# A tile's probabilities turned by two DMA transposes, one for the high and one for the low halves

## The chip, the core and the metric

The kernel runs on one core of a Trainium2 chip. The core has a matmul engine (TensorE, PE in the profile, its weight loads PEld), VectorE (DVE), ScalarE (ACT), GpSimd (POOL) and SyncE (SP), which issues the DMAs; 16 DMA engines move the data. The metric is the device time of one execution in microseconds (us).

## What is computed

Eight batches of 56 query rows of 256 numbers pass two cross-attention layers (16 heads of 128, 1500 context rows and one bias row each), a two-layer MLP, and a gated third cross-attention, the audio attention (16 heads of 16, the context normalised first, with a mask). The core of the reference, with its setup left out:

```python
def _cross_attention(q_in, kv_in, wq, bq, wk, bk, wv, bv, wo, bo, bias_k, bias_v):
    ...
    logits = jnp.einsum('bqhk,bthk->bhqt', qh, kh) / scale
    weights = jax.nn.softmax(logits, axis=-1)
    ctx = jnp.einsum('bhqt,bthk->bqhk', weights, vh).reshape(b, q_len, H * K)
    return ctx @ wo + bo
...
res = x
h = _layer_norm(x, ln1_scale, ln1_offset)
x = res + _cross_attention(h, xf_1, wq1, bq1, wk1, bk1, wv1, bv1, wo1, bo1, bias_k1, bias_v1)
res = x
h = _layer_norm(x, ln2_scale, ln2_offset)
x = res + _cross_attention(h, xf_2, wq2, bq2, wk2, bk2, wv2, bv2, wo2, bo2, bias_k2, bias_v2)
h = _layer_norm(x, ln_mlp_scale, ln_mlp_offset)
h = jax.nn.gelu(h @ w_fc1 + b_fc1, approximate=False) @ w_fc2 + b_fc2
...
a = _layer_norm(audio_kv, ln_gamma, ln_beta)
...
scores = jnp.einsum('bhtd,bhsd->bhts', Q, K) * scale
scores = jnp.where(mask, scores, jnp.float32(-jnp.inf))
attn = jax.nn.softmax(scores, axis=-1)
out = jnp.einsum('bhts,bhsd->bhtd', attn, V)
...
return hidden_states + jnp.tanh(gate) * out
```

## The kernel before

Numbers that enter a matmul are split in a high and a low half of 16 bits, and a product is made of three matmuls (high by high, high by low, low by high). In the first two attentions the queries are first taken through the keys' weights, so that scores and averages are made with the context itself. The 16 x 56 = 896 rows of heads and queries of a batch are 7 tiles (RT) of 128 rows; 8 batches make 56 tiles a layer (TILES). The 1500 context rows are 12 blocks (NT) of 128, the last of 92.

A tile t goes through these steps, each engine with its own order written out by hand:

1. TensorE makes the scores (`scores`), 3 parts of 6 matmuls and a one-column one, in three PSUM banks; odd and even tiles have their own.
2. VectorE takes the maxima (`maximum`, `row_maximum`, L1347, L1378), ScalarE the exponentials (`exponentiate`, L1071), into `prob`.
3. ScalarE writes the high half of the probabilities into `ph[:, i, 0:TC]` (`probs_high`, L1080), VectorE the low half into `ph[:, i, TC:2*TC]` (`probs_low`, L1403); i is t % 2.
4. SyncE turns both halves, 24 blocks of 128 x 128, by one DMA transpose into `pT` (`turn_probs`, L468).
5. TensorE makes the average (`weigh`): 12 blocks with three matmuls each, 36 in all.
6. ScalarE and VectorE write the average's halves (`average_high` L1089, `average_low` L1297), and SyncE turns them by a transpose of 4 blocks into the queries' place (`turn_average`, L476).

TensorE's loop over x runs scores of tile x and then the average of tile x - 2 (LAG). VectorE's slot x makes the maxima of tile x, with the low half of tile x - 1 between its first and its second part. SyncE's slot x turns tile x - 1, then the average of tile x - 3, and then issues loads of the context: DMAs of one queue, issued in this order, each behind the waits of those ahead. After tile 55 ScalarE waits for both last transposes before it splits four weight slices (L1039, L1263 on VectorE), since their place holds `ph` and `pT`. Then the column of the bias row goes round through memory (`tokT`, `scratch`, `ptok`), and the output projection begins.

The audio attention has 7 tiles for each of 8 batches as well. There `audio_maximum` (L1354) adds the mask and takes the maximum, `audio_exponentiate` is L1124, `audio_high` (L1133) writes `aph[:, i, 0:TC]`, `audio_low` (L1372) the low half, `turn_audio` (L508) turns both into `probT`, and `audio_average` makes 24 matmuls for a window of four heads (224 columns), four windows a batch. Between them run the units (keys and values of the next batch: TensorE, then L1117 and L1411), whose keys are turned by `turn_keys` (L499), 12 blocks at a time. SyncE's slot y holds the keys, the probabilities of tile y - 1, a piece of context (L445) and, in the slot of tile 4, the next batch's mask (`mask_load`, L460), right behind the transpose of tile 3. ScalarE turns the mask into a row (`mask_row`, L1138, and `mask_addend`, L1144) in the slot of tile 5, with small steps of VectorE between (L1436 to L1445), and VectorE's maximum of tile 6 comes after them.

## Time and profile before

| what | us |
|---|---|
| median of 3 runs | 1602.12 (1599.8 to 1603.47) |
| the profiled execution | 1609.13 |
| its span, from the first to the last instruction | 1607.4 |
| TensorE busy | 1470.9 (92%) |
| VectorE busy | 1020.2 (63%) |
| ScalarE busy | 833.2 (52%) |
| GpSimd busy | 480.5 (30%) |
| DMA engines, mean share | 74% in the queue of the kernel's DMAs |

The first attention runs from about 72 to 519 us, the second from 644 to 1093, the audio attention from 1208 to the end; projections, norms and the MLP lie between. A busy TensorE is at work for its whole span, and only what shortens its waits there can shorten the run; where it is idle, the row tells who released it. Times of a timeline count from the span's start.

### The profile page before, as it was taken

How to read it: one execution, taken by the hardware profiler on the slowest of the kernel's cores; microseconds unless marked ns; L12 is line 12 of the kernel's file. 1: busy time of each engine (PE TensorE's matmuls, PEld its weight loads, DVE VectorE, ACT ScalarE, POOL GpSimd, SP SyncE). 2: the span in 40 equal slices, each digit the busy share in tenths (PEclk: the TensorE clock that was granted, in tenths of full speed). 3: DMA queues.
4: the chain of work that ended last, by engine and by line, in shares of the span. 5: the costliest groups of instructions: out<-in, count | busy, mean ns of one | idle time of the engine just before them, and what ended most of it. 6: DMA issues, size and time to landing. Idle time of an engine off the chain costs nothing.

```text
span 1607.4 us, 24281 instructions
## 1 busy us (share of the span) xinstructions
PE 1470.9 (92%) x9170; PEld 889.3 (55%) x9170; DVE 1020.2 (63%) x2150; ACT 833.2 (52%) x1437; POOL 480.5 (30%) x456
## 2 busy tenths in 40 slices
PE   7989999999998989899999999998988887898875
PEld 3356666666665333566666666663443444444443
DVE  6755555556555347656666666653467787898885
ACT  4644455544454336455445554443345666666663
POOL 4424233423331200333342334200014444434300
PEclk9999999999999889999999999997999999999998
DMA  5198988988897210798889889884115989999886
GB/s 197 51 197 183 174 172 181 188 156 183 178 187 143 81 65 14 173 183 168 178 179 180 171 176 189 155 166 117 53 30 116 185 174 183 196 192 180 168 146 126
DMA packets 664704, 246.50 MB, mean 153 GB/s; under 512 B 637452, under 2 KB 638972, under 8 KB 664588
## 3 DMA queue, kind: packets, MB, share of 16 engines
q1 hardware_dynamic: 664588, 244.95, 74.2%
q8 instruction: 73, 1.20, 0.3%
q14 instruction: 43, 0.35, 0.1%
HBM read 84.94 MB, written 0.52 MB: 53 GB/s over the span
## 4 chain that ended last, share of the span: by engine, by line
PE 78%; DVE 10%; DMA 5%; ACT 3%; SPq 2%; issue 1%; ACTq 0%; DVEq 0%
PE SC L684 44%; PE PV L684 34%; DVE prob L1354 2%; DVE qc L1372 2%; SPq L508 2%; DVE core L1411 2%; DMA core<-qc 2%; DMA mask<-in_mask_dram 2%; DMA core<-core 1%; ACT rowbuf L1138 1%; DVE core L1403 1%; DVE core L1263 0%; ACT qc L1133 0%; DMA qc<-core 0%; ACT prob L1071 0%
## 5 line engine op out<-in xcount | busy, mean ns | idle before, releaser
L684 PE MATMUL PV<-core 128*128 128x256 f16 (+1 forms) x4800 | 546.6, 273 | 40.1 <-DMA core<-qc 16.4
L684 PEld LDWEIGHTS PV<-core 128*128 128x128 f16 x4800 | 463.7, 99 | 111.9 <-issue 19.3
L1071 ACT ACTIVATE prob<-SC,nmax 128x500 f32<-128x500 f32 x336 | 223.9, 675 | 430.7 <-DVE nmax L1378 430.7
L684 PE MATMUL SC<-ctxT,qc 128*128 128x500 f16 x2016 | 443.1, 374 | 2.6 <-DVE qc L1282 2.6
L1347 DVE TENSOR_REDUCE mx<-SC 128x1 f32<-128x500 f32 x336 | 225.0, 670 | 328.2 <-PE SC L684 328.2
L684 PEld LDWEIGHTS SC<-ctxT,qc 128*128 128x128 f16 x2016 | 195.5, 97 | 210.1 <-DVE qc L1282 3.5
L1403 DVE SCALAR_TENSOR_TENSOR core<-prob,core 128x1500 f16<-128x1500 f32 x112 | 200.0, 1786 | 8.2 <-ACT core L1080 8.2
L616 POOL CAST ctxT<-stage 128x750 f16<-128x750 f32 x64 | 53.1, 830 | 465.2 <-DMA stage<-in_ctx_t_dram 240.7
L1080 ACT ACTIVATE core<-prob 128x1500 f16<-128x1500 f32 x112 | 162.9, 1454 | 3.5
L684 PE MATMUL SC<-ctxT 128*128 128x512 f16 x576 | 143.0, 395 | 14.5 <-DVE core L1411 14.4
L684 PE MATMUL SC<-qc 128*128 128x512 f16 x480 | 118.8, 394 | 40.1 <-DVE mx L1354 40.1
L1124 ACT ACTIVATE prob<-prob,nmax 128x1500 f32<-128x1500 f32 x56 | 86.4, 1543 | 46.4 <-DVE nmax L1358 46.4
L1133 ACT ACTIVATE qc<-prob,rsc 128x1500 f16<-128x1500 f32 x56 | 86.4, 1544 | 42.6 <-DVE rsc L1365 29.1
L636 POOL CAST ctxT<-stage 128x768 f16<-128x768 f32 x32 | 27.6, 861 | 270.7 <-DMA stage<-in_ctx_p_dram 145.0
L1354 DVE CUSTOM_DVE_ANT_0 prob<-SC,rowbuf 128x1500 f32<-128x1500 f32 x56 | 95.9, 1712 | 18.7 <-PE SC L684 18.7
L1372 DVE SCALAR_TENSOR_TENSOR qc<-prob,rsc,qc 128x1500 f16<-128x1500 f32 x56 | 100.8, 1799 | 10.9 <-ACT qc L1133 10.9
L616 POOL CAST core<-stage 128x768 f16<-128x768 f32 x64 | 56.2, 878 | 169.2 <-DMA stage<-in_ctx_nat_dram 169.2
L684 PEld LDWEIGHTS SC<-ctxT 128*128 128x128 f16 x576 | 57.4, 101 | 89.2 <-issue 29.8
L618 POOL TENSOR_TENSOR core<-stage,core 128x768 f16<-128x768 f32 x64 | 105.1, 1643 | 5.1
L618 POOL TENSOR_TENSOR ctxT<-stage,ctxT 128x750 f16<-128x750 f32 x64 | 101.8, 1590 | 5.1
L684 PEld LDWEIGHTS SC<-qc 128*128 128x128 f16 x480 | 46.2, 99 | 101.4 <-issue 53.8
L1411 DVE SCALAR_TENSOR_TENSOR core<-SC,rstd,core 128x256 f16<-128x256 f32 x192 | 83.3, 476 | 18.2 <-ACT core L1117 18.2
(138 smaller groups left out, 1364.5 us busy)
## 6 DMA issues: line engine op xcount, KB each, us to landing
stage<-in_ctx_nat_dram SPq DMA_DIRECT2D x64, 384.0 KB, 3.9
stage<-in_ctx_t_dram SPq DMA_DIRECT2D x64, 375.0 KB, 3.5
stage<-in_ctx_p_dram SPq DMA_DIRECT2D x32, 384.0 KB, 3.8
core<-in_wq_dram SPq DMA_DIRECT2D x8, 512.0 KB, 3.6
core<-in_wk_dram SPq DMA_DIRECT2D x8, 512.0 KB, 3.7
core<-in_wv_dram SPq DMA_DIRECT2D x8, 512.0 KB, 4.2
core<-in_wo_dram SPq DMA_DIRECT2D x8, 512.0 KB, 4.4
qc<-core SPq DMA_TRANSPOSE x144, 2.5
```

Source lines behind the costliest of these rows:

```text
L616: nc.gpsimd.tensor_copy(hi, src).then_inc(split_hi, 1)
L618: nc.gpsimd.tensor_tensor(lo, src, hi, ALU.subtract).then_inc(stage_free, 1)
L684: return nc.tensor.matmul(o, a, c, start=start, stop=stop, skip_group_check=skip)
L1071: nc.scalar.activation(prob[:, i, c * CW:c * CW + w], SETS[i][c][:, 0:w], ACT.Exp, bias=nmax[:, i, :], accum_out=sum3[:, i, c:c + 1]).then ...
L1080: nc.scalar.activation(ph[:, i, 0:T], prob[:, i, 0:T], ACT.Copy, scale=UP).then_inc(ph_hi, 1)
L1124: nc.scalar.activation(prob[:, i, 0:T], prob[:, i, 0:T], ACT.Exp, bias=nmax[:, i, :], accum_out=sum3[:, i, 0:1]).then_inc(as_exp, 1)
L1133: nc.scalar.activation(aph[:, i, 0:T], prob[:, i, 0:T], ACT.Copy, scale=rsc[:, y % 4, 1:2]).then_inc(aph_hi, 1)
L1347: nc.vector.tensor_reduce(mx3[:, t % 2, c:c + 1], SETS[t % 2][c][:, 0:w], AX_X, ALU.max)\
L1354: nc.vector.tensor_tensor_reduce(out=prob[:, i, 0:T], in0=scores_of(y), in1=maskb[:, b % 2, :], scale=1.0, scalar=-3.0e38, op0=ALU.add, op ...
L1372: nc.vector.scalar_tensor_tensor(aph[:, i, TC:TC + T], prob[:, i, 0:T], rsc[:, y % 4, 1:2], aph[:, i, 0:T], ALU.mult, ALU.subtract).then_i ...
L1403: nc.vector.scalar_tensor_tensor(ph[:, i, TC:TC + T], prob[:, i, 0:T], UP, ph[:, i, 0:T], ALU.mult, ALU.subtract).then_inc(ph_lo, 1)
L1411: ins = nc.vector.scalar_tensor_tensor(lo[:, i, :, :], src[:, i, :, :], rstd[:, n:n + 1], hi[:, i, :, :], ALU.mult, ALU.subtract)
```

## The change

`ph` and `aph` are turned by two transposes of 12 blocks instead of one of 24. SyncE issues the one of the high halves as soon as ScalarE has written them (`ph_hi`, `aph_hi`), then waits for the low halves and issues the other. Each has its own semaphores (`pth_full`, `ptl_full`, `apth_full`, `aptl_full`). TensorE's average waits for the high ones, runs all matmuls with them (24 of 36, in the audio stage 12 of 24), then waits for the low ones and runs the rest. ScalarE's wait before it overwrites a high half is for the high transpose alone, and VectorE gets the wait for the low one.

```diff
@@ def turn_probs(t): @@
-                sp.wait_ge(ph_lo, t + 1)
+                sp.wait_ge(ph_hi, t + 1)
                 if t >= 2:
                     sp.wait_ge(pv_done, t - 1)
-                sp.dma_start_transpose(pT[:, i, :, :], ph[:, i, :]).then_inc(pt_full[i], 16)
+                sp.dma_start_transpose(pT[:, i, 0:NT, :], ph[:, i, 0:TC]).then_inc(pth_full[i], 16)
+                sp.wait_ge(ph_lo, t + 1)
+                sp.dma_start_transpose(pT[:, i, NT:2 * NT, :], ph[:, i, TC:2 * TC]).then_inc(ptl_full[i], 16)
@@ def turn_audio(y): @@
-                sp.wait_ge(aph_lo, y + 1)
+                sp.wait_ge(aph_hi, y + 1)
                 if b > 0:
                     sp.wait_ge(apv_done, NW * (b - 1) + LAST_WINDOW[s] + 1)
-                sp.dma_start_transpose(probT[:, :, s * P:(s + 1) * P], aph[:, i, :]).then_inc(apt_full[i], 16)
+                sp.dma_start_transpose(probT[:, 0:NT, s * P:(s + 1) * P], aph[:, i, 0:TC]).then_inc(apth_full[i], 16)
+                sp.wait_ge(aph_lo, y + 1)
+                sp.dma_start_transpose(probT[:, NT:2 * NT, s * P:(s + 1) * P], aph[:, i, TC:2 * TC])\
+                    .then_inc(aptl_full[i], 16)
@@ def weigh(l, x): @@
-                pe.wait_ge(pt_full[i], 16 * (t // 2 + 1))
+                pe.wait_ge(pth_full[i], 16 * (t // 2 + 1))
                 if t >= 2:
                     pe.wait_ge(av_lo, t - 1)
                 for j in range(NT):
                     w = width(j)
-                    for n, (pi, ci) in enumerate(((0, 0), (1, 0), (0, 1))):
-                        ins = mm(PV[i][:, 0:D], pT[0:w, i, pi * NT + j, :], nat[0:w, par, ci, j, :],
-                                 j == 0 and n == 0, j == NT - 1 and n == 2)
+                    for ci in range(2):
+                        mm(PV[i][:, 0:D], pT[0:w, i, j, :], nat[0:w, par, ci, j, :], j == 0 and ci == 0, False)
+                pe.wait_ge(ptl_full[i], 16 * (t // 2 + 1))
+                for j in range(NT):
+                    w = width(j)
+                    ins = mm(PV[i][:, 0:D], pT[0:w, i, NT + j, :], nat[0:w, par, 0, j, :], False, j == NT - 1)
                 ins.then_inc(pv_done, 1)
@@ def audio_average(b, w): @@
-                for i in range(2):
-                    pe.wait_ge(apt_full[i], 16 * ((y + 2 - i) // 2))
...
-                for j in range(NT):
-                    r = width(j)
-                    for i in range(2):
+                for i in range(2):
+                    for k in range(2):
+                        pe.wait_ge((apth_full, aptl_full)[i][k], 16 * ((y + 2 - k) // 2))
+                    for j in range(NT):
+                        r = width(j)
                         ins = mm(PV[w % 2][:, 0:WR], values(NT * b + j, w)[0:r, :],
                                  probT[0:r, i * NT + j, w * WR:(w + 1) * WR], j == 0 and i == 0, j == NT - 1 and i == 1)
@@ ScalarE, probs_high(t); audio_high(y) likewise with apth_full @@
                 if t >= 2:
-                    act.wait_ge(pt_full[i], 16 * (t // 2))
+                    act.wait_ge(pth_full[i], 16 * (t // 2))
@@ ScalarE, attention(l), x == TILES @@
-                            act.wait_ge(pt_full[i], 16 * (TILES // 2) * (l + 1))
+                            act.wait_ge(pth_full[i], 16 * (TILES // 2) * (l + 1))
+                            act.wait_ge(ptl_full[i], 16 * (TILES // 2) * (l + 1))
@@ VectorE, probs_low(t); audio_low(y) likewise with aptl_full @@
                 dve.wait_ge(ph_hi, t + 1)
+                if t >= 2:
+                    dve.wait_ge(ptl_full[i], 16 * (t // 2))
```

On SyncE's queue, the start of the first layer's attention, before: the transposes of tiles 0 to 3 (`core<-core`), with context and weights between, and the first turned averages (`qc<-core`).

```order
L421 DMA core<-in_wv_dram 128x1024 [waits w_lo]
L468 DMA_TRANSPOSE core<-core 128x24x128 [waits ph_lo]
L445 DMA stage<-in_ctx_nat_dram 128x768 [waits stage_free] x2
L421 DMA core<-in_wo_dram 128x1024 [waits w_lo]
L468 DMA_TRANSPOSE core<-core 128x24x128 [waits ph_lo]
```

The same place now:

```order
L423 DMA core<-in_wv_dram 128x1024 [waits w_lo]
L470 DMA_TRANSPOSE core<-core 128x12x128 [waits ph_hi]
L472 DMA_TRANSPOSE core<-core 128x12x128 [waits ph_lo]
L447 DMA stage<-in_ctx_nat_dram 128x768 [waits stage_free] x2
L423 DMA core<-in_wo_dram 128x1024 [waits w_lo]
L470 DMA_TRANSPOSE core<-core 128x12x128 [waits ph_hi]
L472 DMA_TRANSPOSE core<-core 128x12x128 [waits ph_lo]
```

Two transposes stand where one stood; nothing has changed its place.

On TensorE, tile 0's average in the first layer (`PV<-core`), behind the scores of tile 2, before:

```order
L684 MATMUL SC<-ctxT,qc 128x500 [waits exp_done]
L684 MATMUL SC<-ctxT,qc 128x500 x5
L684 MATMUL SC<-one,rowbuf 128x1
L684 MATMUL PV<-core 128x256 [waits pt_full0,stage_free]
L684 MATMUL PV<-core 128x256 x35
```

And now:

```order
L691 MATMUL SC<-ctxT,qc 128x500 x5
L691 MATMUL SC<-one,rowbuf 128x1
L691 MATMUL PV<-core 128x256 [waits pth_full0,stage_free]
L691 MATMUL PV<-core 128x256 x23
L691 MATMUL PV<-core 128x256 [waits ptl_full0]
L691 MATMUL PV<-core 128x256 x11
```

The 36 matmuls have been parted into 24 behind the high transpose and 12 behind the low one.

On SyncE's queue in the audio stage, the slots of tiles 3 and 4 of a batch (`qc<-core` are the keys, `core<-qc` the probabilities, `stage` a piece of context), before:

```order
L499 DMA_TRANSPOSE qc<-core 128x12x128 [waits as_score,m_lo]
L508 DMA_TRANSPOSE core<-qc 128x24x128 [waits apv_done,aph_lo]
L445 DMA stage<-in_ctx_p_dram 128x768 [waits stage_free]
L499 DMA_TRANSPOSE qc<-core 128x12x128 [waits as_score,m_lo]
L508 DMA_TRANSPOSE core<-qc 128x24x128 [waits apv_done,aph_lo]
L460 DMA mask<-in_mask_dram 128x1500 [waits mask_ready]
L499 DMA_TRANSPOSE qc<-core 128x12x128 [waits as_score,m_lo]
```

And now:

```order
L503 DMA_TRANSPOSE qc<-core 128x12x128 [waits as_score,m_lo]
L512 DMA_TRANSPOSE core<-qc 128x12x128 [waits apv_done,aph_hi]
L514 DMA_TRANSPOSE core<-qc 128x12x128 [waits aph_lo]
L447 DMA stage<-in_ctx_p_dram 128x768 [waits stage_free]
L503 DMA_TRANSPOSE qc<-core 128x12x128 [waits as_score,m_lo]
L512 DMA_TRANSPOSE core<-qc 128x12x128 [waits apv_done,aph_hi]
L514 DMA_TRANSPOSE core<-qc 128x12x128 [waits aph_lo]
L462 DMA mask<-in_mask_dram 128x1500 [waits mask_ready]
L503 DMA_TRANSPOSE qc<-core 128x12x128 [waits as_score,m_lo]
```

The mask still stands behind tile 3's low half, now with 12 blocks instead of 24 directly ahead of it.

## Rows read from the trace of the kernel before

**Rows 1.** The page, its first line.

```profile
span 1607.4 us, 24281 instructions
```

**Rows 2.** Windows: stretch, length, busy us (instructions) by engine, clock, DMA share, GB/s.

```profile
200.00:300.00 100.00, 100.00 (x710) 68.19 (x709) 55.99 (x129) 50.76 (x104) 36.04 (x30) 1.00 0.88 177
1400.00:1500.00 100.00, 83.55 (x483) 46.60 (x482) 81.88 (x163) 68.79 (x77) 46.25 (x58) 0.97 0.96 188
```

**Rows 3.** Line L499, the keys' transposes: issue ns min/median/max, then landing.

```profile
L499 SPq DMA_TRANSPOSE qc<-core x32: 1391/1432/2553, 1172.0 to 1539.9; - x32
...
DMA to landing us min/median/max: 3.6/4.5/6.2
```

**Rows 4.** Windows amid a lone 24-block and a lone 12-block transpose.

```profile
84.30:85.30 1.00, 0.00 (x0) 0.00 (x0) 0.15 (x1) 1.00 (x5) 0.00 (x0) 1.00 1.15 212
...
1174.00:1174.50 0.50, 0.34 (x2) 0.22 (x3) 0.50 (x2) 0.50 (x1) 0.00 (x0) 1.00 1.17 216
```

**Rows 5.** Timeline, both layers' first tiles: start, length, engine, line, what [idle before <-releaser].

```profile
80.59 1.72 DVE L1403 SCALAR_TENSOR_TENSOR core<-prob,core 128x1500 f16<-128x1500 f32 x1 [1.33 <-ACT core L1080]
...
88.09 6.94 PE L684 MATMUL PV<-core 128*128 128x256 f16 x36 [4.41 <-DMA core<-core]
...
652.89 2.93 DVE L1403 SCALAR_TENSOR_TENSOR core<-prob,core 128x1500 f16<-128x1500 f32 x1 [1.33 <-ACT core L1080]
...
657.22 0.16 DVE L1378 TENSOR_REDUCE nmax<-mx 128x1 f32<-128x3 f32 x1
...
661.51 6.95 PE L684 MATMUL PV<-core 128*128 128x256 f16 x36 [5.53 <-issue]
...
664.64 0.16 DVE L1378 TENSOR_REDUCE nmax<-mx 128x1 f32<-128x3 f32 x1
```

**Rows 6.** Window of tile 0's average in the second layer.

```profile
661.50:668.30 6.80, 6.79 (x37) 4.97 (x38) 3.27 (x7) 3.43 (x7) 4.88 (x4) 0.57 1.07 299
```

**Rows 7.** Timeline, both layers' last tiles.

```profile
508.93 3.66 SPq L468 DMA_TRANSPOSE core<-core  x1
...
514.62 4.11 PE L684 MATMUL PV<-core 128*128 128x256 f16 x36 [2.35 <-DMA core<-core]
514.64 2.19 ACT L1039 ACTIVATE core<-core 128x512 f16<-128x512 f32 x4 [7.13 <-issue]
515.30 2.50 DVE L1263 SCALAR_TENSOR_TENSOR core<-core 128x512 f16<-128x512 f32 x4 [5.68 <-ACT core L1039]
...
519.26 0.48 DVE L1297 SCALAR_TENSOR_TENSOR core<-PV,rsc,core 128x256 f16<-128x256 f32 x1 [1.07 <-ACT core L1089]
...
1082.25 3.70 SPq L468 DMA_TRANSPOSE core<-core  x1
...
1093.89 0.48 DVE L1297 SCALAR_TENSOR_TENSOR core<-PV,rsc,core 128x256 f16<-128x256 f32 x1 [2.37 <-ACT core L1089]
```

**Rows 8.** Waits: engine, line, waited for: us in total, times, longest.

```profile
ACT rowbuf L1138 <- DMA mask<-in_mask_dram: 21.4, 7, 3.7
```

**Rows 9.** The chain that ended last, audio stage: first and last of seven such pieces.

```profile
1247.32 3.99 SPq L508
...
1535.20 3.97 SPq L508
```

**Rows 10.** Timeline, the mask in the audio stage's third batch.

```profile
1343.99 4.34 SPq L508 DMA_TRANSPOSE core<-qc  x1
...
1352.20 1.45 ACT L1138 ACTIVATE rowbuf<-mask 128x1500 bf16<-128x1500 uint8 x1 [3.70 <-DMA mask<-in_mask_dram]
...
1356.28 2.16 PE L684 MATMUL SC<-qc 128*128 128x512 f16 x6 [3.42 <-DVE mx L1354]
```

**Rows 11.** Timeline, the last tile of the audio stage.

```profile
1585.53 1.54 ACT L1133 ACTIVATE qc<-prob,rsc 128x1500 f16<-128x1500 f32 x1 [1.64 <-DMA core<-qc]
1587.11 1.78 DVE L1372 SCALAR_TENSOR_TENSOR qc<-prob,rsc,qc 128x1500 f16<-128x1500 f32 x1 [1.80 <-ACT qc L1133]
...
1591.27 6.97 PE L684 MATMUL PV<-core 128*128 128x224 f16 x48 [8.01 <-DMA core<-qc]
```

More of the change, by code:

```diff
@@ L228, in build @@
         aph_lo = sem("aph_lo")
-        apt_full = [sem(f"apt_full{k}") for k in range(2)]
+        apth_full = [sem(f"apth_full{k}") for k in range(2)]
+        aptl_full = [sem(f"aptl_full{k}") for k in range(2)]
         apv_done = sem("apv_done")
@@ L285, in build @@
         ph_lo = sem("ph_lo")
-        pt_full = [sem(f"pt_full{k}") for k in range(2)]
+        pth_full = [sem(f"pth_full{k}") for k in range(2)]
+        ptl_full = [sem(f"ptl_full{k}") for k in range(2)]
         av_hi = sem("av_hi")
@@ L1371, in audio_low @@
                 dve.wait_ge(aph_hi, y + 1)
+                if y >= 2:
+                    dve.wait_ge(aptl_full[i], 16 * (y // 2))
                 nc.vector.scalar_tensor_tensor(aph[:, i, TC:TC + T], prob[:, i, 0:T], rsc[:, y % 4, 1:2], aph[:, i, 0:T],
```

2 lines of the change are left out of this document (1 added, 1 removed).

## The prediction

> **What bounds the kernel now.** I read four views, in this order. First the page's span and the windows by stage: the profiled execution spans 1607.4 us [rows 1], and inside an attention layer TensorE is busy for all of a 100 us window, at clock 1.00, while in the last stage (the audio attention, from about 1208 us) it is busy for 83.55 of 100 and the DMA engines for 0.96 [rows 2]. So inside a layer nothing that comes earlier can help: the 36 + 18 matmuls of a tile set its period, 7.75 us. What can move is where TensorE stands still: the first tiles of a layer, its last tiles, and the audio stage. Second, the DMA transposes, issue and landing [rows 3, 4]. Third, the timeline at those places [rows 5, 7, 10, 11], with the clock [rows 6]: the reader is to follow one tile there from ScalarE's high half over VectorE's low half and SyncE's transpose to TensorE. Fourth, the waits and the chain in the audio stage [rows 8, 9].
>
> **The change part by part.** One transpose of 24 blocks of 128x128 becomes two of 12. 168 tiles do that (56 in each of three attentions). The matmuls, their shapes and the weight loads stay the same in number; only their order changes, so TensorE's own work costs nothing more. The kernel has a 12-block transpose already, that of the audio keys: it holds SyncE 1.43 us and lands 3.6 us after its issue at best, 4.5 in the median of a crowded stage [rows 3]. Its data move at 216 GB/s, against 212 for a 24-block one [rows 4]; so a half costs half the DMA time, and twice 1.43 us of issue is less than the 4 us a whole one takes [rows 9]. I take 3.7 us to landing for a half on a quiet queue.
>
> The notes on the chip speak against the halves at one point: the Trainium skill, page "DMA: Bandwidth & Descriptors", section "Latency and other measured facts", says that a DMA transpose whose reads cannot be joined to 4 KB or more loses about 30%. A half reads 3 KB from each partition where the whole read 6 KB. By the page each half would take some 0.55 us more and the sum below would shrink by about 6 us; the row of the 12-block transpose, with the same 3 KB, shows no such loss.
>
> *First tiles of a layer.* TensorE has done the scores of tiles 0 to 2 and waits for tile 0. In the second layer VectorE starts the low half at 652.89 (so the high half is there) and needs 2.93 us; the transpose goes out at 655.8 and tile 0's 36 matmuls start at 661.51, after 5.53 us of idling, that is, from 655.98 [rows 5]. They then need 6.95 us instead of 4.11 [rows 7], because the clock is at 0.57 of full speed (between the two levels, 1.2 and 2.4 GHz) after the idle time [rows 6]. After the change: high half out at 652.9, landed 656.6; 24 matmuls at 4.11/36 = 0.114 us end at 659.3; low half out at 655.8, landed 659.5, 12 matmuls end at 660.9. TensorE idles 0.6 us instead of 5.5, so I count full clock. Before, 661.51 + 6.95 = 668.46: gain 7.5. First layer likewise: high half at 80.59, landed 84.3, end of the high matmuls 87.0, low half out at 82.3, landed 86.0, end 88.4, against 88.09 + 6.94 = 95.03: gain 6.6 [rows 5]. Is the head start kept? Next late is the softmax loop over VectorE and ScalarE: its row maxima follow each other in 664.64 - 657.22 = 7.4 us [rows 5], shorter than TensorE's 7.75, and tile 3's exponentials are due only when TensorE reaches tile 5 (660.9 + 16.3 = 677.2; they would start at about 672). So it is kept; I take off 1 us for small waits: **13 us**, bounds 10 and 14.
>
> *Last tiles.* Tile 55's transpose goes out at 508.93 and lands at about 514.6: at 514.62 its matmuls start and at 514.64 ScalarE starts four weight slices that wait for the same landing [rows 7]. After: the low half lands at 508.93 + 3.9 = 512.8 (the high half has left just ahead). TensorE's end moves from 518.73 to about 515.0. But ScalarE's and VectorE's weight work moves by only 1.8 us, and behind it come two averages: from the landing 3.2 us to VectorE's last weight slice (515.30 + 2.50 - 514.64), then twice 0.48: tile 55's low average begins at 516.5 instead of 519.26. Gain 2.7, not 3.7. In the second layer the issue is at 1082.25 and the low average begins at 1093.89; by the same steps 1082.25 + 3.9 + 3.2 + 0.5 = 1089.8: gain 4.1 [rows 7]. Together **6.8 us**, bounds 4 and 8. The token row's round trip through memory starts behind these averages and shifts with them.
>
> *Audio stage: the mask.* Here the change acts on something that it does not name. SyncE issues the mask of the next batch right behind tile 3's transpose. The chain that ended last passes there seven times: low half written, SyncE busy for 3.63 to 4.42 us with the 24-block transpose, then the mask's landing, ScalarE, VectorE, scores [rows 9]. In the third batch: the issue ends at 1343.99 + 4.34, the mask goes out, ScalarE starts at 1352.20 after 3.70 us of waiting, TensorE at 1356.28 after 3.42 us [rows 10]. ScalarE waits 21.4 us for the mask in all [rows 8]. Now only the low half stands between the written low half and the mask. The seven issues sum to 27.7 us; with 7 x 1.43 instead the mask comes 17.7 us earlier in sum; where the high half still fills the queue, the second half of a whole one (3.99 - 1.43 = 2.56) is the nearest price, and 9.8 remain. I take **15 us**, nearer the first, since the high half is out about 2 us before. Behind the wait nothing else is late at once: the scores that VectorE then reads have been done for 3 us.
>
> *Audio stage: the end.* ScalarE waits for the transpose of two tiles back (1.64 us at the last tile), VectorE's last low half is at 1587.11, and TensorE's averages start at 1591.27 after 8.01 us of idling and take 6.97 us for 48 matmuls, cold [rows 11]; they end at 1598.24. After: last low half 1.7 us earlier, done at 1587.2, landed at 1591.3, and only 12 matmuls (1.2 us warm, 2.4 cold) behind it, with window 2 done before: 1593 to 1595. **4 us**, bounds 1.7 and 5.7.
>
> What is added: ScalarE and VectorE each wait for their own half's transpose of two tiles ago, which is never later than the wait for the whole; no price. On SyncE behind the new wait for the high half stand the low half, the turned average, loads and keys; none of them can go earlier than before in any case, and they are no later.
>
> Sum: 13 + 6.8 + 15 + 4 = 38.8 us. The profiled execution took 1609.1 us, 7 above the median of the runs, 1602.1; the median becomes 1602.1 - 38.8 = **1563.3 us**.
>
> **The rivals.** *Layers only.* The mask's head start is taken back: DMA engines at 0.96 [rows 2] and keys of 12 blocks in the same queue could make the mask's data land as late as now, or TensorE meets the next wait of that batch. For it: the share; against it: a batch moves 216 blocks of 32.8 KB and 1.8 MB of loads, 8.9 MB, which at 216 GB/s need 41 us of its (1535.20 - 1247.32)/6 = 48 us [rows 4, 9]. Time: 1602.1 - 19.8 = 1582.
>
> *SyncE becomes the bound (slower).* If a half held SyncE far longer than the keys' 1.43 us, because both halves queue on each other, the queue would set a tile's period. In the audio stage SyncE is held 27.7 us of a batch's 48 by seven wholes, 5.7 by four keys and some 3 by five plain loads; 11.6 are free, 1.65 for each tile, so the point is a half of (3.95 + 1.65)/2 = 2.8 us. At 3.0 every tile costs 0.4 us, in the layers by a like account 0.3: 168 x 0.3 = 50, less 20 at the layers' ends: 1632. Against it: [rows 3] with 1.43 in the median, 2.55 at most.
>
> *Nothing moves.* The low half alone decides everywhere: the halves' data interleave and both land when the whole did. Then 24 of 36 matmuls wait as long as before: 1600. Against it: the landing of a 12-block transpose grows with its own size.
>
> **How the numbers follow.** Forecast 0.64, layers only 0.20, more than forecast (mask gain up to ScalarE's 21.4 us, ends at their bounds: 1602.1 - 49.1 = 1553) 0.05, nothing 0.05, slower 0.06. Range: from 1550, below the upper bounds' sum, to 1584, just past layers only; it leaves out less than 0.2. Within 0.2% (3.2 us, what a measurement of this kernel can tell from no change) 0.05; slower 0.06; faster 0.89.
>
> **What would show it.** Starts: tile 0's matmuls begin 5 us earlier in both layers, split into 24 and 12, and the clock stays up. Inside a layer: 7.75 us a tile, unchanged. Ends: the low average 2.7 and 4.1 us earlier, counted from the last scores. Audio: low-half issues before the mask near 1.5 us, ScalarE's wait for the mask near 1 us each, batches of 46 us instead of 48. Wrong, if 12-block issues take over 2.5 us in the median, if the DMA's rate falls, or if the batches keep their 48 us.

## The result, and the profile after

| | before | changed |
|---|---|---|
| median of the runs, us | 1602.8 (1599.8 to 1610.4) | 1584.4 (1583.7 to 1589.5) |
| profiled execution, us | 1609.1 | 1584.8 |
| span of that execution, us | 1607.4 | 1583.0 |

The ratio of the runs is 0.9885, with a 95% interval of 0.9845 to 0.9925: 18.4 us less, where 38.8 were forecast. The change is a gain, as forecast, but less than half as large, and the time lies just outside the range. The two profiled executions differ by 24.4 us; most of what follows goes by their traces, since only they show where.

The first line of the page, and below it the windows that answer to [rows 2]: a stretch amid the first layer, and one in the audio stage.

```profile
span 1583.0 us, 24647 instructions
```

```profile
200.00:300.00 100.00, 100.00 (x713) 68.35 (x711) 55.32 (x129) 50.77 (x104) 36.96 (x28) 1.00 0.87 174
1400.00:1500.00 100.00, 87.63 (x506) 48.94 (x504) 86.79 (x169) 68.46 (x77) 49.20 (x48) 0.95 0.93 186
```

Inside a layer nothing moved: TensorE fills all of the 100 us, as it did. In the audio stage it is busy for 87.6 of 100, where it was 83.6.

The half transposes themselves, high and low, of the audio stage: issue in ns, minimum, median, maximum, then the landing. They answer to [rows 3].

```profile
L512 SPq DMA_TRANSPOSE core<-qc x56: 1392/1728/3124, 1214.4 to 1566.9; - x56
```

```profile
L514 SPq DMA_TRANSPOSE core<-qc x56: 1392/1438/2605, 1219.4 to 1568.7; - x56
...
DMA to landing us min/median/max: 3.6/3.8/5.4
```

They cost about what the keys' 12-block transposes cost before (1.43 us). The medians of 1.44 and 1.73 us are far from the 2.8 us at which SyncE would have become the bound, and the earliest landing is the 3.6 us that the keys had.

Next comes one account of the whole execution, cut at five points that every trace has: the first score matmuls of each layer, the bias matmuls of the new token row that end each layer's attention, the start of the audio stage's projection, and VectorE's last addition to xT. All lengths in us, from the timelines.

| stretch | before | changed | gain |
|---|---|---|---|
| start to first scores, first layer | 71.52 | 70.63 | 0.9 |
| first layer's attention | 454.32 | 449.73 | 4.6 |
| to the second layer's scores | 118.02 | 118.44 | -0.4 |
| second layer's attention | 456.57 | 453.10 | 3.5 |
| to the audio stage | 107.63 | 108.67 | -1.0 |
| audio stage | 395.56 | 378.69 | 16.9 |

The audio stage gained about what was forecast for it (19). The two attention layers were to give 19.8 and gave 8.1. **The question is where the layers' 11.7 us went.**

**The layers' starts.** Timeline of the changed kernel, first tiles of the first layer, then tile 0's average and tile 1's in the second; start, length, engine, line, what [idle before <-releaser]. It answers to [rows 5].

```profile
79.69 1.57 SPq L470 DMA_TRANSPOSE core<-core  x1
...
81.44 1.65 SPq L472 DMA_TRANSPOSE core<-core  x1
...
83.79 4.10 PE L691 MATMUL PV<-core 128*128 128x256 f16 x36 [1.00 <-DMA core<-core]
86.61 2.15 SPq L470 DMA_TRANSPOSE core<-core  x1
...
92.75 4.11 PE L691 MATMUL PV<-core 128*128 128x256 f16 x36 [1.06 <-DMA core<-core]
```

```profile
651.60 4.10 PE L691 MATMUL PV<-core 128*128 128x256 f16 x36 [0.67 <-issue]
...
660.12 4.11 PE L691 MATMUL PV<-core 128*128 128x256 f16 x36 [0.62 <-DMA core<-core]
```

The high half goes out when it is written (79.69), TensorE idles 1.0 and 0.7 us in place of 4.4 and 5.5, and tile 0's 36 matmuls take 4.10 us, not 6.95: the clock stays up. The window of the second layer's tile 0 shows it, against 0.57 in [rows 6].

```profile
651.60:655.70 4.10, 4.10 (x37) 3.54 (x38) 1.17 (x5) 3.54 (x7) 0.00 (x0) 1.00 1.00 233
```

Tile 5's scores, counted from tile 0's, come 5.0 us earlier in the first layer and 6.2 in the second. At tile 0's end the gain is larger, 6.2 and 7.7 us, counted in the same way; tile 1's wait (1.06 and 0.62 us) and, in the second layer, one of 0.54 us at tile 2 take a part of it back.

**The layers' ends.** Timeline of the changed kernel at tile 55, first and second layer. It answers to [rows 7].

```profile
507.37 2.19 ACT L1049 ACTIVATE core<-core 128x512 f16<-128x512 f32 x4 [5.67 <-DMA core<-core]
508.03 4.31 DVE L1274 SCALAR_TENSOR_TENSOR core<-core 128x512 f16<-128x512 f32 x4 [4.21 <-ACT core L1049]
509.71 4.50 POOL L665 TENSOR_SCALAR_AFFINE_SELECT core<-core 16x2048 f16<-16x2048 f16 x2 [31.91 <-PE PV L691]
512.27 0.86 DVE L1308 SCALAR_TENSOR_TENSOR core<-PV,rsc,core 128x256 f16<-128x256 f32 x2
```

```profile
1071.19 1.54 SPq L472 DMA_TRANSPOSE core<-core  x1
...
1077.16 1.49 PE L691 MATMUL PV<-core 128*128 128x256 f16 x12 [1.09 <-DMA core<-core]
1077.35 2.19 ACT L1049 ACTIVATE core<-core 128x512 f16<-128x512 f32 x4 [7.58 <-DMA core<-core]
1078.01 6.11 DVE L1274 SCALAR_TENSOR_TENSOR core<-core 128x512 f16<-128x512 f32 x4 [6.12 <-ACT core L1049]
1078.72 4.86 POOL L665 TENSOR_SCALAR_AFFINE_SELECT core<-core 16x2048 f16<-16x2048 f16 x2 [50.87 <-PE PV L691]
1084.05 0.86 DVE L1308 SCALAR_TENSOR_TENSOR core<-PV,rsc,core 128x256 f16<-128x256 f32 x2
```

Four weight slices on VectorE that took 2.50 us before [rows 7] now take 4.31 and 6.11. What is new beside them is GpSimd. Its two affine selects (they spread the bias of the values for the next stage) are released by the last tile's matmuls. The selects now start 2.3 and 1.4 us behind ScalarE's first weight slice, amid VectorE's slices; before it was 4.2 and 5.5 us. Before, the selects started when the slices were through; the same lines of the trace of before:

```profile
515.30 2.50 DVE L1263 SCALAR_TENSOR_TENSOR core<-core 128x512 f16<-128x512 f32 x4 [5.68 <-ACT core L1039]
...
518.80 3.96 POOL L658 TENSOR_SCALAR_AFFINE_SELECT core<-core 16x2048 f16<-16x2048 f16 x2 [33.25 <-PE PV L684]
```

The second block shows another miss: the low half is issued at 1071.19 and ScalarE's slices start at 1077.35, 6.16 us later. In the first layer it is 507.37 - 503.12 = 4.25. The trace has the landings themselves at 5.9 and 4.0 us after the issue.

**The audio stage.** Timeline of the changed kernel, third batch, which answers to [rows 10]; then the waits of ScalarE for the mask [rows 8].

```profile
1331.76 1.81 SPq L514 DMA_TRANSPOSE core<-qc  x1
1333.62 0.61 SPq L462 DMA_DIRECT2D mask<-in_mask_dram  x1
...
1337.60 1.45 ACT L1149 ACTIVATE rowbuf<-mask 128x1500 bf16<-128x1500 uint8 x1 [1.33 <-DMA mask<-in_mask_dram]
...
1341.67 2.71 PE L691 MATMUL SC<-qc 128*128 128x512 f16 x6 [3.36 <-DVE mx L1365]
```

```profile
ACT rowbuf L1149 <- DMA mask<-in_mask_dram: 9.0, 7, 2.6
```

SyncE is held 1.41 to 1.81 us ahead of the mask, 10.8 us over the seven batches, where it was 27.7. ScalarE's wait for the mask falls by 12.4 us, not by 16.9: the mask itself now lands 3.7 to 5.6 us after its issue (29.3 in sum), before 3.3 to 4.2 (24.8). Six batches take 1519.79 - 1241.52 = 278.3 us, or 46.4 each, against 48.0. TensorE still stands 3.36 us ahead of the scores at 1341.67, as before (3.42), and it still runs the next matmuls cold: 2.71 us for six, where a warm six takes 1.46.

Last, the end of the audio stage [rows 11].

```profile
1566.87 1.78 DVE L1385 SCALAR_TENSOR_TENSOR qc<-prob,rsc,qc 128x1500 f16<-128x1500 f32 x1 [0.73 <-ACT qc L1144]
1566.89 5.05 PEld L691 LDWEIGHTS PV<-core 128*128 128x128 f16 x36 [3.87 <-issue]
1566.92 5.28 PE L691 MATMUL PV<-core 128*128 128x224 f16 x36 [3.64 <-issue]
...
1572.56 1.31 PE L691 MATMUL PV<-core 128*128 128x224 f16 x12 [0.37 <-DMA core<-qc]
```

36 of the 48 matmuls are done before the last low half has landed; 12 are left behind it.

### The profile page after: what moved, and what is told of

Same layout as the page of the kernel before. It is cut to its first block, busy times and chain, and to the rows that moved or that the text cites. A ratio compares the mean times of both kernels' runs of the same rounds, so it can differ in the third digit from the quotient of the medians.

```text
span 1583.0 us, 24647 instructions
## 1 busy us (share of the span) xinstructions
PE 1465.8 (93%) x9170; PEld 886.2 (56%) x9170; DVE 1019.3 (64%) x2150; ACT 832.1 (53%) x1437; POOL 530.1 (33%) x456
## 4 chain that ended last, share of the span: by engine, by line
PE 76%; DVE 13%; DMA 4%; ACT 4%; issue 1%; SPq 1%; ACTq 0%; DVEq 0%
PE SC L691 44%; PE PV L691 32%; DVE prob L1365 3%; DVE qc L1385 3%; DVE core L1426 2%; DMA mask<-in_mask_dram 2%; DMA core<-core 1%; DVE core L1274 1%; DVE core L1418 1%; ACT prob L1081 1%; ACT rowbuf L1149 1%; SPq L514 1%; ACT core L1090 1%; DVE mx L1358 0%; ACT qc L1144 0%
## 5 line engine op out<-in xcount | busy, mean ns | idle before, releaser
L691 PE MATMUL PV<-core 128*128 128x256 f16 (+1 forms) x4800 | 539.3, 271 | 11.3 <-DMA core<-core 6.7
L623 POOL CAST ctxT<-stage 128x750 f16<-128x750 f32 x64 | 68.4, 1068 | 449.6 <-PE SC L691 234.8
L1418 DVE SCALAR_TENSOR_TENSOR core<-prob,core 128x1500 f16<-128x1500 f32 x112 | 193.2, 1725 | 17.1 <-ACT core L1090 17.1
L691 PE MATMUL SC<-qc 128*128 128x512 f16 x480 | 122.6, 403 | 39.8 <-DVE mx L1365 39.8
L643 POOL CAST ctxT<-stage 128x768 f16<-128x768 f32 x32 | 42.8, 1338 | 243.8 <-PE SC L691 132.5
L623 POOL CAST core<-stage 128x768 f16<-128x768 f32 x64 | 69.5, 1085 | 143.5 <-DMA stage<-in_ctx_nat_dram 143.5
```

The lines of the kernel that those rows point to most:

```text
L623: nc.gpsimd.tensor_copy(hi, src).then_inc(split_hi, 1)
L691: return nc.tensor.matmul(o, a, c, start=start, stop=stop, skip_group_check=skip)
L1418: nc.vector.scalar_tensor_tensor(ph[:, i, TC:TC + T], prob[:, i, 0:T], UP, ph[:, i, 0:T], ALU.mult, ALU.subtract).then_inc(ph_lo, 1)
```

## The experiments

Each was timed beside the kernel before on the same chip, and the ratio is to that. The medians of before were 1603.6 us beside e1 to e4, 1607.7 beside e5 to e8 and 1607.4 beside e9 to e11, so ratios are compared, and times only between kernels that ran beside the same before.

| kernel | median, us | ratio | 95% interval |
|---|---|---|---|
| e1_before_again | 1603.99 | 0.9997 | 0.9976 to 1.0017 |
| e2_layers_only | 1599.53 | 0.9965 | 0.9949 to 0.9981 |
| e3_audio_only | 1590.32 | 0.9913 | 0.9884 to 0.9943 |
| e4_spread_late | 1577.98 | 0.9824 | 0.9793 to 0.9854 |
| e5_before_mask_early | 1588.52 | 0.9885 | 0.9869 to 0.9901 |
| e6_mask_early | 1570.49 | 0.9774 | 0.9758 to 0.9790 |
| e7_split_late | 1604.18 | 0.9981 | 0.9967 to 0.9994 |
| e8_best | 1564.76 | 0.9745 | 0.9727 to 0.9762 |
| e9_before_spread_late | 1606.76 | 1.0007 | 0.9992 to 1.0022 |
| e10_best_loads | 1570.22 | 0.9768 | 0.9744 to 0.9793 |
| e11_best_again | 1561.93 | 0.9720 | 0.9698 to 0.9743 |

The same account of stretches as above, in us, from the profiled execution of each:

| kernel | first layer | between | second layer | to audio | audio |
|---|---|---|---|---|---|
| before | 454.32 | 118.02 | 456.57 | 107.63 | 395.56 |
| changed | 449.73 | 118.44 | 453.10 | 108.67 | 378.69 |
| e1_before_again | 453.34 | 120.72 | 456.18 | 107.65 | 395.57 |
| e2_layers_only | 449.93 | 117.57 | 453.18 | 104.79 | 397.04 |
| e3_audio_only | 453.17 | 120.64 | 456.08 | 107.65 | 381.31 |
| e4_spread_late | 447.96 | 118.43 | 448.93 | 104.18 | 380.00 |
| e5_before_mask_early | 454.52 | 117.71 | 458.05 | 104.72 | 375.53 |
| e6_mask_early | 449.24 | 117.61 | 452.76 | 107.22 | 367.43 |
| e7_split_late | 452.91 | 120.75 | 455.91 | 105.39 | 398.27 |
| e8_best | 447.80 | 120.75 | 449.50 | 107.58 | 368.04 |
| e9_before_spread_late | 454.25 | 118.57 | 455.27 | 104.58 | 394.26 |
| e10_best_loads | 449.31 | 120.72 | 449.96 | 107.26 | 365.60 |
| e11_best_again | 447.75 | 118.35 | 449.11 | 104.02 | 366.11 |

The columns "between" and "to audio" hold feed-forward work that no edit touches. They vary by 3.2 and 4.7 us from one execution to the next, with the granted clock. The windows of "between" for e1_before_again and of "to audio" for e4_spread_late:

```profile
525.17:645.89 120.72, 112.50 (x494) 46.37 (x494) 61.65 (x102) 55.05 (x100) 4.71 (x4) 0.88 0.15 49
```

```profile
1087.04:1191.22 104.18, 97.17 (x458) 43.68 (x458) 55.40 (x112) 44.33 (x76) 9.87 (x8) 0.93 0.23 64
```

In before the same two stretches had clocks of 0.91 and 0.89. So the difference of two profiled executions is worth no more than the stretches that the edit touches, which is why each experiment is read by its own column. Those have noise as well: the kernels whose audio stage is that of before have 394.3 to 397.0 us there, and those whose layers are that of before 453.2 to 454.5 and 456.1 to 458.1.

### Parts of the change

e1_before_again is before without an edit, to see what two runs of one kernel differ by.

> The kernel before, unchanged, profiled once more. The first profiled execution took 1609.1 us where the median of its runs was 1602.1. If the excess was a matter of that execution alone, this one comes out near 1602 and the difference of 24.4 us between the two traces shrinks to about 18; if the profiled execution is always that much longer, it is near 1609 again. The ratio to the kernel before is 1.000.

It came out at 0.9997. Its profiled execution is again long (span 1609.0 us, median of the runs 1604.0). That is no rule: e9, below, times like before (median 1606.8), and its profiled execution took 1604.0.

e2_layers_only keeps the change in the two attention layers and puts the audio stage back:

```diff
-                sp.wait_ge(aph_hi, y + 1)
+                sp.wait_ge(aph_lo, y + 1)
...
-                sp.dma_start_transpose(probT[:, 0:NT, s * P:(s + 1) * P], aph[:, i, 0:TC]).then_inc(apth_full[i], 16)
-                sp.wait_ge(aph_lo, y + 1)
-                sp.dma_start_transpose(probT[:, NT:2 * NT, s * P:(s + 1) * P], aph[:, i, TC:2 * TC])\
-                    .then_inc(aptl_full[i], 16)
+                sp.dma_start_transpose(probT[:, :, s * P:(s + 1) * P], aph[:, i, :]).then_inc(apt_full[i], 16)
```

> Only the two layers' attentions have the two transposes, the audio attention keeps the one of 24 blocks. My account of the two traces gives the layers 7 us: 5.0 and 6.9 at the starts, and -0.4 and -3.5 at the ends, where a gain of 2.7 and 4.1 was forecast, less about 1 us of the projections. Expected 1595 us, with VectorE's four weight slices at the layers' ends taking 4.3 and 6.1 us in sum instead of 2.5. The forecast's own working would have 1582.

e3_audio_only does the reverse:

```diff
-                sp.wait_ge(ph_hi, t + 1)
+                sp.wait_ge(ph_lo, t + 1)
...
-                sp.dma_start_transpose(pT[:, i, 0:NT, :], ph[:, i, 0:TC]).then_inc(pth_full[i], 16)
-                sp.wait_ge(ph_lo, t + 1)
-                sp.dma_start_transpose(pT[:, i, NT:2 * NT, :], ph[:, i, TC:2 * TC]).then_inc(ptl_full[i], 16)
+                sp.dma_start_transpose(pT[:, i, :, :], ph[:, i, :]).then_inc(pt_full[i], 16)
```

> Only the audio attention has the two transposes. My account of the two traces gives this stage 16.9 us, of which part may be noise of the kernel before: expected 1587 us. The batch's period 46.4 us instead of 48.0, the mask landing later behind its issue (3.7 to 5.6 us) than before (3.3 to 4.2). The forecast's working had 19 us: 1583. The rival that the mask's head start is taken back would have 1598.

By the ratios the layers' half is worth 5.6 us and the audio half 14.0 us; together 19.6, which agrees with the 18.4 of the whole. Both times lie 3 to 5 us above the expected ones, which were taken from the difference of two traces. Each moves only its own columns: the layers' sum falls by 7.8 us in e2, the audio stage by 14.3 in e3. e2 has the long weight slices of the changed kernel, 6.11 us in the second layer, though nothing of the audio part is in it:

```profile
1078.49 6.11 DVE L1270 SCALAR_TENSOR_TENSOR core<-core 128x512 f16<-128x512 f32 x4 [5.86 <-ACT core L1045]
1079.20 4.85 POOL L661 TENSOR_SCALAR_AFFINE_SELECT core<-core 16x2048 f16<-16x2048 f16 x2 [50.14 <-PE PV L687]
```

### GpSimd beside VectorE

e4_spread_late is the changed kernel with one more wait on GpSimd: the selects start only when VectorE has written the layer's last low average, which stands behind its weight slices.

```diff
+                pool.wait_ge(av_lo, TILES * (l + 1))
```

> The changed kernel, with one more wait on GpSimd: its affine selects of the values' bias (16 partitions x 2048, two of them, 4.5 to 4.9 us) at a layer's end start behind the last low average instead of behind the last average matmul. Theory: since the last average now ends before VectorE's weight slices, GpSimd runs beside these and slows them; then the four slices take 2.5 us again, the last low average comes 1.8 us earlier in the first layer and 3.6 in the second, and the run takes 5 us less than the changed kernel, about 1579 us. Rival: the slices are slowed by the DMA writes of the turned averages or by anything else at that place; then they stay at 4.3 and 6.1 us and the run is unchanged or slower by the wait.

e9_before_spread_late puts the same wait into the kernel before, where the selects come behind the slices anyway.

> A control: the kernel before, with the one wait that e4_spread_late has (GpSimd's selects behind the layer's last low average). In before the selects start at 518.80 us, behind the weight slices anyway, so if the cost that e4 took away is the overlap of the selects with VectorE's slices, this changes nothing: ratio to before 0.998 to 1.002. If the selects cost something by themselves in either order, or the wait helps in another way, this gains as e4 did, 5 to 6 us (ratio 0.996).

Timeline of e4_spread_late at the end of the second layer:

```profile
1076.83 2.50 DVE L1275 SCALAR_TENSOR_TENSOR core<-core 128x512 f16<-128x512 f32 x4 [5.91 <-ACT core L1050]
1079.25 0.87 DVE L1309 SCALAR_TENSOR_TENSOR core<-PV,rsc,core 128x256 f16<-128x256 f32 x2
1080.24 3.96 POOL L666 TENSOR_SCALAR_AFFINE_SELECT core<-core 16x2048 f16<-16x2048 f16 x2 [53.33 <-issue]
```

The slices are back at 2.50 us and the selects at 3.96. The layers' attention is 1.8 and 4.2 us shorter than in the changed kernel. The ratio is 0.0061 lower, but the two intervals overlap a little; the firmer pair is e8_best against e6_mask_early below, which differ by this wait alone and ran beside the same before: 1564.8 and 1570.5 us, with layers 1.4 and 3.3 us shorter. In before the wait changes nothing (1.0007, the interval holds 1). So it is the overlap that costs, not the selects by themselves. **A wait that was added made the kernel faster.**

The overlap has a shape. One slice alone takes 0.63 us at the least; the longest in each trace, and each select, are these (ns, minimum, median, maximum), first the changed kernel, then before:

```profile
L1274 DVE SCALAR_TENSOR_TENSOR core<-core x72: 627/684/2497, 10.3 to 1169.4; 128x512 f16<-128x512 f32 x72
```

```profile
L665 POOL TENSOR_SCALAR_AFFINE_SELECT core<-core x4: 2087/2446/2448, 509.7 to 1081.1; 16x2048 f16<-16x2048 f16 x4
```

```profile
L1263 DVE SCALAR_TENSOR_TENSOR core<-core x72: 630/685/1382, 10.2 to 1179.4; 128x512 f16<-128x512 f32 x72
```

```profile
L658 POOL TENSOR_SCALAR_AFFINE_SELECT core<-core x4: 1997/2000/2002, 518.8 to 1095.4; 16x2048 f16<-16x2048 f16 x4
```

The longest slice takes 2.50 us, about as long as a select. In the first layer the slices cost 4.31 - 2.50 = 1.81 us more, in the second 6.11 - 2.50 = 3.61, twice as much: one slice stood for a select there, two here. A narrow timeline of the second layer shows one such pair by itself; the slice begins while the second select is at work and ends 0.55 us behind it (1084.12 against 1083.57), which is about what a slice takes alone:

```profile
1081.13 2.44 POOL L665 TENSOR_SCALAR_AFFINE_SELECT core<-core 16x2048 f16<-16x2048 f16 x1
1081.64 2.48 DVE L1274 SCALAR_TENSOR_TENSOR core<-core 128x512 f16<-128x512 f32 x1
```

The Trainium skill, page "SBUF — State Buffer", section "Who interferes with whom", says that the two engines share a port pair, that this pair is an exclusive lock, and that a VectorE instruction with two inputs in SBUF contends there with a GpSimd instruction that reads SBUF. The slice does read two SBUF tiles and the select one, and the trace agrees, with 1.81 us for each select that a slice stood for. The select pays too, 2.45 for 2.00 us.

GpSimd's other work in the changed kernel grew as well: its 128 x 768 copies of the context take 1085 ns in the mean where they took 878, and it is busy for 530.1 us instead of 480.5. It is off the path there, and no run shows that this costs time.

### The mask

The edit of e5_before_mask_early (to before) and of e6_mask_early (to the changed kernel) is the same: SyncE issues the next batch's mask ahead of tile 3's transpose (in the changed kernel, of both its halves) instead of behind it.

```diff
+                if s == 4 and b + 1 < B:
+                    mask_load(b + 1)
                 if y > 0:
                     turn_audio(y - 1)
...
-                if s == 4 and b + 1 < B:
-                    mask_load(b + 1)
```

> The kernel before, with one edit: in each audio batch SyncE issues the next batch's mask load ahead of the DMA transpose of the tile that it used to stand behind. Theory M (the audio part's loss before is ScalarE's wait for the mask row behind a long transpose, and its size is that wait, 21.4 us in the trace of before): the wait goes nearly whole, the batch period falls from 47.98 us to about 45.5, and the time by 14 to 19 us, to 1585 to 1590, although no transpose is split. Rival N (the audio part gained from the split transposes themselves, whose high halves land earlier): the mask's place is worth little, under 6 us, 1597 or more. The mask's own landing should be 3.3 us again, as in before, if what lengthened it to 3.7 to 5.6 in the changed kernel is a queue full of half transposes; it then shows less than the changed kernel's sum of 29.3 us for the seven.

> The changed kernel, with the mask load issued ahead of both halves. Theory M: ScalarE's remaining wait for the mask row (9.0 us over seven batches, 2.6 the longest) goes, and the time falls by 5 to 9 us below the changed kernel's 1584.4, to 1575 to 1579. Rival N: ScalarE's wait only passes to the next one in the batch (its wait for the row maximum, 63.4 us in sum in the changed kernel), and the time stays at 1582 to 1586.

With no transpose split at all, e5 gains as much as the whole change (ratio 0.9885 both); its audio stage is 20.0 us shorter than before's. ScalarE no longer waits for the mask in either. So the mask's place behind a transpose was the largest of the losses that the change touched. One part of e5's expectation failed: the mask's landing did not stay at 3.3 us, its median is 4.8, with no half transpose of probabilities in the queue. Why it grew is open; it no longer matters, since nobody waits for it.

e6 gained more than expected, 17.8 us by the ratios and 11.3 in its audio column. Where from is told by TensorE's busy time in the audio stage. The windows of the whole stage come in this order: before, changed, e5, e6.

```profile
1208.06:1603.62 395.56, 319.69 (x1783) 176.75 (x1784) 316.46 (x619) 249.02 (x277) 135.21 (x160) 0.95 0.87 168
```

```profile
1200.57:1579.26 378.69, 319.56 (x1783) 177.15 (x1784) 318.04 (x620) 248.35 (x277) 153.65 (x160) 0.95 0.91 176
```

```profile
1206.63:1582.16 375.53, 313.77 (x1783) 176.03 (x1784) 315.13 (x619) 248.34 (x277) 140.30 (x160) 0.97 0.91 177
```

```profile
1197.53:1564.96 367.43, 314.65 (x1783) 175.28 (x1784) 316.98 (x619) 247.49 (x277) 160.08 (x160) 0.97 0.96 181
```

The changed kernel has 16.7 us less idle time on TensorE than before (395.56 - 319.69 against 378.69 - 319.56) and the same busy time. In e5 and e6 the busy time falls as well, by 5.9 and 5.0 us against before, for the same 1783 matmuls, at clock 0.97 in place of 0.95. The place to look is each batch's pause. Windows right behind TensorE's wait for the scores that the mask holds up, third batch, before, changed and e6:

```profile
1356.20:1363.20 7.00, 6.92 (x25) 2.82 (x26) 5.67 (x10) 5.26 (x5) 1.66 (x4) 0.76 0.43 81
```

```profile
1341.60:1348.60 7.00, 6.93 (x25) 2.88 (x26) 5.67 (x10) 5.15 (x5) 5.28 (x8) 0.76 0.84 157
```

```profile
1334.00:1341.00 7.00, 6.32 (x29) 2.79 (x30) 5.67 (x10) 5.25 (x5) 7.00 (x10) 1.00 1.06 199
```

After 3.42 and 3.36 us of idling the granted clock of the next 7 us is 0.76, between the levels of 1.2 and 2.4 GHz; in e6 TensorE idles 1.32 us there and the clock stays at 1.00. The third batch is a clear case, and the others are less so. The same pause and the clock of the 7 us behind it in the first six batches:

| kernel | pause, us | granted clock behind it |
|---|---|---|
| before | 3.32, 3.36, 3.42, 2.29, 3.29, 3.07 | 0.57, 0.76, 0.76, 0.76, 0.76, 1.00 |
| changed | 2.45, 3.10, 3.36, 4.65, 3.95, 2.73 | 0.76, 1.00, 0.76, 0.76, 0.63, 0.80 |
| e6 | 1.92, 1.52, 1.32, 1.92, 2.62, 1.92 | 1.00, 1.00, 1.00, 1.00, 0.76, 0.76 |

Five of six are cold in before and in the changed kernel, two of six in e6. The length of the pause alone does not decide it: 3.10 us left the clock up once, 1.92 us left it up twice and not the third time. The changed kernel made ScalarE's wait for the mask shorter, but TensorE's pauses there did not shrink (it came to the place earlier, since its waits for the transposes ahead of it, 1.3 to 3.0 us a batch before, were gone), and so it kept the cold matmuls. The 11.3 us of e6's audio column are 6.4 of idle time and 4.9 of clock. The rest of the 17.8 is no part of that column; the interval of the changed kernel's ratio alone is 13 us wide.

### Split or early

e7_split_late keeps both halves but issues them together, when the low half is written.

```diff
-                sp.wait_ge(ph_hi, t + 1)
+                sp.wait_ge(ph_lo, t + 1)
...
-                sp.wait_ge(aph_hi, y + 1)
+                sp.wait_ge(aph_lo, y + 1)
```

> The changed kernel, but both halves of each tile's transpose wait for the low half, so the transposes are split and in the changed order, and none is issued early. If the early issue of the high halves makes the gains at the layers' starts and behind the last audio tile, they go: tile 0's PV lands as before (S(5) of the first layer about 39 us behind S(0), as in before, and not 33.8), and the time is near 1600 (1596 to 1604). If it is the split itself (a first half lands sooner than the whole), about half of the gain stays: 1590 to 1594. The mask load stands behind two half transposes that are issued together, so ScalarE's mask wait should be at least the 21.4 us of before.

Ratio 0.9981: 3 us of the 18 come from the split. Tile 0's matmuls start 2.73 us late in place of 4.41, at full clock:

```profile
86.53 4.09 PE L691 MATMUL PV<-core 128*128 128x256 f16 x36 [2.73 <-DMA core<-core]
```

The audio stage is 2.7 us longer than before's, with 25.8 us of waiting for the mask, as two halves stand ahead of it. What counts in the change is that the high half leaves early.

### Both edits, and the loads

e8_best has both edits, the later selects and the earlier mask, on the changed kernel.

> The changed kernel with both edits: GpSimd's selects wait until the weight slices at the end of each layer are through (the earlier run e4_spread_late, 1578.0 us), and the mask load goes ahead of the halves. The two act in different stages and should add: by theory M 1569 to 1573; by rival N 1576 to 1579.

> e8_best once more, on the same chip as the other two, as what e10 is compared with: the ratio to before should come out as 0.9745 again, within 0.002 (1563 to 1570 us).

It came out at 0.9745 and, once more, at 0.9720: 1561.9 us, 45 below before and the fastest of all here. The repeat missed by a little the 0.002 that was allowed to it. The two edits add: 0.0061 and 0.0111 off the changed kernel's 0.9885 would give 0.9713. The time lies under theory M's 1569 to 1573, as e6 had already come out 5 us under what was expected of it; the clock's 4.9 us, which the expectations did not have, are of that size.

e10_best_loads asks about what the starts and the last landing fell short by. It moves the context loads of slots 1 and 55 one slot on, behind the transposes that they stood ahead of.

```diff
+                    if x in (2, TILES):
+                        loads(B * l + (x - 1) // RT, (x - 1) % RT)
                     if x < TILES:
-                        loads(B * l + b, s)
+                        if x not in (1, TILES - 1):
+                            loads(B * l + b, s)
```

> e8_best, with the context loads of the layers' tile slots 1 and 55 issued one slot later, behind the transposes of tiles 1 and 55 in place of ahead of them. Theory Q (what the starts and ends fell short by is the landing behind loads that share the 16 engines): W(1)'s wait of 0.85 us at the first layer's start goes, the second layer's last low half lands 3.9 us after its issue and not 5.9, so the last average comes 1 to 2 us earlier; 2 to 4 us in all against e8_best, ratio about 0.0015 to 0.0025 lower than the other run of this call. Rival: the landing is set by the transposes' own data, which keep all engines busy at 200 to 217 GB/s; the waits stay, and so does the time (ratio the same within 0.001).

No gain, but a loss: 0.9768 against e11's 0.9720, with intervals that do not meet, so that neither the theory's gain nor its rival's equal time came. Both layers are longer than in e11, by 1.6 and 0.9 us. Timeline of e10, tiles 1 and 2, and of e11, tile 1:

```profile
92.36 4.09 PE L695 MATMUL PV<-core 128*128 128x256 f16 x36
...
102.15 4.11 PE L695 MATMUL PV<-core 128*128 128x256 f16 x36 [1.89 <-DMA core<-core]
```

```profile
93.12 4.11 PE L692 MATMUL PV<-core 128*128 128x256 f16 x36 [0.73 <-DMA core<-core]
```

Tile 1's wait is gone, so the loads did cause it; but four loads now stand ahead of tile 2, which waits 1.89 us. The load only chooses the tile that pays. At the second layer's end theory Q fell: without the load the last low half still took 1080.44 - 1075.10 = 5.3 us to its matmuls, not 3.9 (e11: 1075.48 - 1069.81 = 5.7). The rest of the 0.0048 between the two ratios stays open: in the stretches that no edit touches e10's profiled execution was 2.4 and 3.2 us longer than e11's.

## Why the prediction was wrong, point by point

The sum of 38.8 us was worked out on the trace of before, so it is held against the 24.4 us between the two traces. Here are the 14.4 us that are missing, term by term:

| term | forecast | measured | how |
|---|---|---|---|
| layers' starts | 13 | 11.2 | tile 5's scores, 5.0 and 6.2 |
| layers' ends | 6.8 | -3.1 | 4.6 - 5.0 and 3.5 - 6.2 |
| mask | 15 | 12.4 | ScalarE's wait, 21.4 to 9.0 |
| audio tail | 4 | 4.5 | what is left, 16.9 - 12.4 |
| stretches that no edit touches | 0 | -0.6 | 0.9 - 0.4 - 1.0, from run to run |

**Starts: right, a little large.** The mechanism, the split into an early high half, the clock and the kept head start all came as worked out: tile 0's average ends 6.2 and 7.7 us earlier, where 6.6 and 7.5 were forecast. The "1 us for small waits" was too little; tile 1's waits and tile 2's in the second layer took 2.7 us (13.9 - 11.2).

**Ends: the step that failed** is "ScalarE's and VectorE's weight work moves by only 1.8 us, and behind it come two averages: from the landing 3.2 us to VectorE's last weight slice". The prediction carried a duration over from before (2.50 us for four slices) as if it belonged to VectorE alone. The matmuls that the change makes earlier also release GpSimd, and its selects moved into the slices. From the landing to the last slice it is 508.03 + 4.31 - 507.37 = 5.0 us and 1078.01 + 6.11 - 1077.35 = 6.8, not 3.2. The slices alone make 1.8 + 3.6 = 5.4 us of it, and e4 gave 1.8 + 4.2 back. The second failed term is the landing, "lands at 508.93 + 3.9", and likewise in the second layer: to ScalarE's start it was 4.25 us and 6.16, so 2.6 more in sum; its cause is open. Some 2 us more lie between the last low average and the bias matmuls: 6.6 us in both layers before, 7.7 and 7.5 after. The last two averages now run back to back, so the two that are turned last leave together, and the token row's DMA goes out 2.6 us behind the last low average instead of 1.75; that this is the reason was not tried. 5.4 + 2.6 + 2 makes 10.0, and the ends fell short by 9.9.

**Mask: right mechanism, size off by 2.6.** It lies within the bounds of 9.8 and 17.7. The issue ahead of the mask became 16.9 us shorter in sum, close to the 17.7 of the upper bound. What the sum left out is that the mask's own landing could grow; it did, by 4.5 us. And it stopped at ScalarE. TensorE's pause was not followed to its end: in most batches it also costs the clock behind it. With the pause left standing that part of the loss stayed, and 5 to 6 us of TensorE's busy time went only when the wait was removed, in e5 and e6.

**Tail: right.** Measured directly, from the last mask's issue to the end, it is 64.4 us before and 59.5 in the changed kernel, 4.9 less; the 4.5 of the table are what the mask's term leaves over. e5 and e6, which have no wait for the mask, differ there by 4.4 us (68.9 and 64.5).

**From trace to median.** The sum was made against a profiled execution of 1609.1 us, and its gain was taken off the median as it stood. Before's profiled execution is 6.3 us above its median, the changed kernel's 0.4; of the 24.4 us between the traces 18.4 remain between the medians. Why is open. e9's profiled execution, of a kernel that times like before, was 5.2 us shorter than before's: 2.5 of that lies in the stretches that no edit touches, and 1.3 each in the second layer and the audio stage. So the 24.4 us are likely a few us too many, and the forecast, which took a trace's gain off a median, missed the measured median by 21.1 us.

**The rivals.** "Layers only" gave 1582, near the measured time, and is wrong all the same: it kept the layers' gain and took the mask's, and the runs show the reverse. SyncE did not become the bound (1.44 and 1.73 us in the median, not 2.8). That nothing moves is refuted by the starts. A half of the layers lands 3.6 us after its issue at best and a whole of before 5.5, so the 12 blocks more cost 1.9 us, and the rates of [rows 4] were 216 and 212 GB/s. The Trainium skill, page "DMA: Bandwidth & Descriptors", section "Latency and other measured facts", puts a loss of about 30% on a transpose whose reads cannot be joined to 4 KB. The trace does not agree: no such loss shows between reads of 3 KB and of 6 KB. None of the rivals had an engine off the path that is released early and gets in the way of one that is on it.

## What to carry over

When a change makes an event earlier, list everything that waits for it, the engines off the critical path too, and ask of each what it will now run beside: here a wait that holds GpSimd back until VectorE is through gave back 5 to 6 us. Look for small transfers that stand in a queue behind large ones: moving one line was worth as much as the whole change. Follow a pause of TensorE to the matmuls behind it: here the change shortened another engine's wait, TensorE's pause stayed, and with it most of the matmuls at a low clock behind it.

## What the runs showed of the hardware

- A slice on VectorE with two SBUF inputs that met GpSimd's select took 2.50 us in place of 0.63 to 0.69, and the select 2.45 for 2.00.
- A DMA transpose of 12 blocks with 3 KB read per partition held SyncE for 1.44 to 1.73 us in the median and landed after 3.6 us at best; one of 24 blocks held it for 3.65 to 3.67 us and landed after 5.4.
- The mask's load of 187.5 KB landed after 3.7 to 5.6 us in the changed kernel and after 3.3 to 4.2 before.
- TensorE's granted clock over the 7 us behind a pause was 0.57 to 0.80 in 12 of 18 places with pauses of 1.9 to 4.7 us, and 1.00 in the other six, with 1.3 to 3.1 us.
- Why the second layer's last low half landed only after 5.9 us, and the first layer's after 4.0, is open. The load ahead of it is not the reason: without it (e10) the matmuls still started 5.3 us after the issue.
